# Causal attention in a two-layer block: 512-query groups per head replaced by head pairs, 256-query groups and split value and output projections

## The reference, cut to what matters

```python
qs = (x @ wq_sem).reshape(b, sl, 16, 64);  ksem = (x @ wk_sem).reshape(b, sl, 16, 64)
qg = _rope((x @ wq_geo).reshape(b, sl, 16, 64)); kg = _rope((x @ wk_geo).reshape(b, sl, 16, 64))
v = (x @ wv).reshape(b, sl, 16, 128)
g = sigmoid(gate_logit)[None, :, None, None]
scores = g * (qs . ksem) * 64**-0.5 + (1 - g) * (qg . kg) * 64**-0.5
attn = softmax(where(causal, scores, -1e9))
out = (attn @ v).reshape(b, sl, 16 * 128) @ wo
```

## Time and profile before

| | us |
|---|---|
| median of 3 runs | 1966.86 |
| profiled execution | 1968.04 |
| its span, first to last instruction | 1966.4 |
| TensorE busy | 1781.5 (91%) |
| DVE busy | 1106.4 (56%) |
| ACT busy | 972.0 (49%) |
| GpSimd busy | 802.1 (41%) |

### The profile page before, as it was taken

One profiled execution on the slowest core, in us unless ns is written; L12 is line 12 of the kernel. 1 busy time (PEld: TensorE's weight loads), 2 busy tenths in 40 slices (PEclk: granted clock), 3 DMA queues, 4 the chain that ended last, 5 costly groups with the idle time before them and its releaser, 6 DMA issues. The chain is left out here.

```text
span 1966.4 us, 33208 instructions
## 1 busy us (share of the span) xinstructions
PE 1781.5 (91%) x9018; PEld 1315.6 (67%) x9018; DVE 1106.4 (56%) x2157; ACT 972.0 (49%) x2052; POOL 802.1 (41%) x788
## 2 busy tenths in 40 slices
PE   6399988439999999999999999999999999999998
PEld 2256656427777777777777777777776677677777
DVE  4799953695546455554645454555544333334467
ACT  4599923015555555555555455555554344444322
POOL 1489931333433444343434434443432233222354
PEclk9599999559999999999999999999999999999999
DMA  4753258200000000000000000000101999999623
GB/s 138 287 183 105 98 154 261 84 3 20 9 20 16 21 8 19 16 20 7 16 21 8 19 16 21 8 19 16 39 9 31 286 313 314 308 315 321 192 87 97
DMA packets 99216, 192.94 MB, mean 98 GB/s; under 512 B 15332, under 2 KB 59620, under 8 KB 96596
## 3 DMA queue, kind: packets, MB, share of 16 engines
q1 hardware_dynamic: 57684, 108.76, 18.0%
q0 software_dynamic: 17152, 47.67, 7.5%
q10 hardware_dynamic: 24336, 35.98, 5.5%
HBM read 140.84 MB, written 51.51 MB: 98 GB/s over the span
## 5 line engine op out<-in xcount | busy, mean ns | idle before, releaser
L1175 POOL TENSOR_TENSOR sw<-sw,rope_t 64x512 f32<-64x512 f32 x128 | 164.3, 1283 | 611.9 <-ACT sw L995 611.9
L1078 DVE TENSOR_TENSOR t<-ps,rope_t 128x512 f32<-128x512 f32 x128 | 88.5, 692 | 363.5 <-ACT sw L995 363.4
L890 PE MATMUL ps<-pt,v 128*128 128x512 f32 (+3 forms) x768 | 270.1, 495 | 19.8 <-DVE xr L1095 17.8
L987 ACT ACTIVATE pb<-ps,negmax 128x128 f32<-128x128 f32 (+7 forms) x256 | 191.1, 747 | 177.1 <-DVE negmax L1063 177.0
L1063 DVE TENSOR_REDUCE negmax<-ps 128x1 f32<-128x128 f32 (+7 forms) x256 | 191.9, 750 | 78.1 <-PE ps L849 76.1
L890 PEld LDWEIGHTS ps<-pt,v 128*128 128x128 f32 x768 | 139.1, 191 | 121.4 <-issue 79.5
L541 POOL DMA_DIRECT2D w2r<-in_w x148 | 77.5, 523 | 326.1 <-PE ps L590 306.3
L1178 POOL TENSOR_TENSOR t<-t,sw 64x512 f32<-64x512 f32 x128 | 179.1, 1399 | 33.6 <-POOL sw L1175 17.9
L883 PE MATMUL ps<-ident,pb 128*128 128x128 f32 x1152 | 171.3, 276 | 23.6 <-ACT pb L987 23.4
L974 ACT COPY pt<-ps 128x512 f32<-128x512 f32 (+3 forms) x256 | 130.1, 508 | 102.0 <-PE ps L883 94.5
L883 PEld LDWEIGHTS ps<-ident,pb 128*128 128x128 f32 x1152 | 133.8, 141 | 68.1 <-ACT pb L987 45.1
(11 more groups left out here) (198 smaller groups left out, 3677.2 us busy)
## 6 DMA issues: line engine op xcount, KB each, us to landing
w13r<-in_w SPq DMA_DIRECT2D x124, 352.0 KB, 6.0
w2r<-in_w POOLq DMA_DIRECT2D x148, 176.0 KB, 6.0
result<-yy ACTq DMA_DIRECT2D x148, 128.0 KB, 5.1
crow<-c_rows SPq DMA_DIRECT2D x32, 512.0 KB, 3.6
t<-sorted SPq DMA_DIRECT2D x124, 128.0 KB, 5.5
sorted<-zeros ACTq DMA_DIRECT2D x15, 1024.0 KB, 16.9
hc<-in_w SPq DMA_DIRECT2D x24, 352.0 KB, 5.3
wraw<-in_wqkv SPq DMA_DIRECT2D x16, 384.0 KB, 3.3
```

Of the source, the lines that this page charges most:

```text
L890: last = pe.matmul(ps[:, 6, c0:512], v[:, buf, j], pt[g][:, j, c0:512], start=j == 0, stop=j == 4 * g + 3)
L987: act.activation(pb[:, qt % 2, 0:cols], ps[:, bank:bank + 2, :].rearrange("p a n -> p (a n)")[:, 0:cols], ACT.Exp, bias=negmax[:, par, qn: ...
L1175: g.tensor_tensor(sw[64:128, p % 2, :], sw[64:128, p % 2, :], rope_t[64:128, 1, (p // 2) * 512:(p // 2 + 1) * 512], ALU.mult).then_inc(s_t ...
```

## The change

- **Order.** A pair of heads is taken together: head 1 and head 2 of the first sequence, then of the second (`body(hp, c, ...)`, c = 0 to 3, hh = c % 2 is the head in the pair). There are still 32 passes of eight steps.
- **Values** are computed for a pair: four fills of bank 7, each of two token tiles by 256 columns, split, in steps 0, 1, 4 and 7 of the pair's first pass. DVE copies them out. The weights of a pair are loaded and split together.
- **Output product** for 256 queries at a time, in steps 2, 4 and 6 and in step 0 of the next pass, plain float32 as before. Its result is taken out of PSUM in two parts, `otr` by ACT and `otl` by DVE.
- **Output projection** in steps 3, 5 and 7 and in step 1 of the next pass, now split, with weights split by DVE.
- **Copies of probabilities** are all ACT's, and stand behind the next exponential instead of before it.
- **`rest`**, the low part of q and k, goes from DVE to GpSimd, interleaved with `rotate`.
- **Memory**: the ring `w2r1` shares memory with attention, so GpSimd waits for the last addition of attention before it loads there.

The core of the diff:

```diff
         def heads_loop(eng, body):
...
+            def four(hp, ends):
+                for c in range(4):
+                    body(hp, c, ends and c == 3)
...
-            def v_half(half, bank, target_b, s_fill):
-                for i in range(4):
-                    t0 = target_b * SEQ + (half * 4 + i) * P
+            def values(m, b, fill):
+
+                pe.wait_ge(s_e7, fill - 1)
+                for a in range(2):
+                    t0 = b * SEQ + (2 * m + a) * P
+                    o = ps[:, 7, a * 2 * P:(a + 1) * 2 * P]
                     for c in range(DC):
-                        last = pe.matmul(ps[:, bank, i * P:(i + 1) * P], xnT1[:, c, t0:t0 + P], wv[:, c], start=c == 0, stop=c == DC - 1)
-                last.then_inc(s_fill, 1)
+                        last = three(pe, o, xnr[:, c, t0:t0 + P], xnl[:, c, t0:t0 + P], wvr[:, c], wvl[:, c], c == 0, c == DC - 1)
+                last.then_inc(s_b7, 1)
...
+            def output(it, g, hh):
+
+                w(pe, s_e6, output_fill(it, g) - 1)
+                pe.wait_ge(s_pl, CHUNKS * it + (2, 4, 8, 12)[g])
+                hd = slice(hh * P, (hh + 1) * P)
+                for j in range(2 * g + 2):
+                    c0 = P if j == 2 * g + 1 else 0
+                    last = pe.matmul(ps[:, 6, c0:2 * P], v[:, j, hd], pt[g % 2][:, j, c0:2 * P], start=j == 0, stop=j == 2 * g + 1)
+                last.then_inc(s_b6, 1)
...
+            def project_out(it, g, slot):
+
+                pe.wait_ge(s_e6, project_fill(it, g) - 1)
                 for a in range(2):
-                    sl = slice((2 * (which % 2) + a) * P, (2 * (which % 2) + a + 1) * P)
-                    last = pe.matmul(ps[:, 6, a * D:(a + 1) * D], ot[:, sl], wo[:], start=True, stop=True)
+                    sl = slice(a * P, (a + 1) * P)
+                    last = three(pe, ps[:, 6, a * D:(a + 1) * D], otr[:, sl], otl[:, sl], wor[:, slot], wol[:, slot], True, True)
                 last.then_inc(s_b6, 1)
...
         def att_act(act):
...
                 for qt in range(8):
+                    if qt < 7 or not last:
+                        exp_tile(it, qt + 1, hh)
                     probs(it, qt)
-                    if qt < 7 or not last:
-                        exp_tile(it, qt + 1, b)
...
         def att_dve(dve):
...
-            def rest(n, p, buf):
-                dve.wait_ge(s_qr, n + 1)
-                o = (slice(None), buf, p % 2, slice((p // 2) * 512, (p // 2 + 1) * 512))
-                dve.tensor_tensor(qkl[o], t1[:, p % 2, :], qkr[o].bitcast(F32), ALU.subtract).then_inc(s_ql, 1)
...
+            def output(it, g):
+                dve.wait_ge(s_otr, 4 * it + g + 1)
+                dve.tensor_tensor(otl[:], ps[:, 6, 0:2 * P], otr[:].bitcast(F32), ALU.subtract).then_inc(s_e6, 1)
...
         def att_pool(g):
...
-            def rotate(it, p):
+            def rotate(it, p, fill):
                 n = 4 * it + p
+                w(g, s_ql, n if p == 0 else n - 1)
                 g.wait_ge(s_a7, n + 1)
...
+            def rest(it, p, buf):
+                g.wait_ge(s_rot, 4 * it + min(p + 2, 4))
+                g.wait_ge(s_qr, 4 * it + p + 1)
+                o = (slice(None), buf, p % 2, slice((p // 2) * 512, (p // 2 + 1) * 512))
+                g.tensor_tensor(qkl[o], t1[:, p % 2, :], qkr[o].bitcast(F32), ALU.subtract).then_inc(s_ql, 1)
...
                 if not last:
                     for p in range(4):
-                        rotate(it + 1, p)
+                        rotate(it + 1, p, piece_fill(2 * hp + c // 2, c % 2, p))
+                        if p:
+                            rest(it + 1, p - 1, 1 - c % 2)
+                    rest(it + 1, 3, 1 - c % 2)
...
             att_pool(g)
+            g.wait_ge(s_e6, ALL_OUTPUTS)
             experts_pool(g, R1, shared_splits(g))
```

More of the change, by code:

```diff
@@ L930, in body @@
                     if qt < 6:
-                        scores(it, qt + 2, b)
+                        scores(it, qt + 2, hh)
                     elif not last:
[L933 to L951, removed]
@@ L952, in body @@
-                    if qt == 7 and not last:
-                        pe.wait_ge(s_e6, use6(it, VHALF) - 1)
-                        v_half(1, 6, 1 - b, s_b6)
-                        pe.wait_ge(s_e7, use7(it, 4) - 1)
-                        v_half(0, 7, 1 - b, s_b7)
+                        scores(it, qt + 2, 1 - hh)
+                    if qt == 0 and not first(it):
+                        if hh == 1:
+                            pe.wait_ge(s_e7, value_fill(pair, 3))
+                        output(it - 1, 3, 1 - hh)
@@ L957, in att_pe @@
+                    if qt in PIECE and not last:
+                        p = PIECE[qt]
+                        if qt == 2 and next_b == 0:
+                            pe.wait_ge(s_ws, 2 * hp + c // 3 * 2 + (1 - hh) + 1)
+                        piece(p, next_b, 1 - hh, piece_fill(pair, hh, p))
             heads_loop(pe, body)
-            for part in range(2):
-                output1(ITS, 0, part)
-            for which, n in ((2, W2), (3, W3)):
-                project_out(which, use6(ITS, n))
+            output(ITS - 1, 3, 1)
@@ L1155, in body @@
[L1155 to L1164 removed]
+                        output(it - 1, 3)
@@ new lines, in body @@
+                    if qt == 1 and not first(it):
+                        add_out(it - 1, 3, prev_b, 1 - hh)
+                    if qt in (2, 4, 6):
+                        output(it, qt // 2 - 1)
+                    if qt in (3, 7):
+                        invert(it, qt // 7, hh)
+                    if qt in (3, 5, 7):
+                        add_out(it, qt // 2 - 1, b, hh)
+                    if qt in VALUE and hh == 0:
+                        values(VALUE[qt], value_fill(pair, VALUE[qt]))
@@ L1165, in att_dve @@
+                    if qt == 4 and c == 3 and not last_pair(hp):
+                        dve.wait_ge(s_b6, project_fill(it - 1, 3))
+                        split_wo(2 * hp + 2, 0)
+                    if qt == 4 and c == 0 and not first(it):
+                        dve.wait_ge(s_b6, project_fill(it - 1, 3))
+                        split_wo(2 * hp + 1, 1)
             heads_loop(dve, body)
-            for which, n in ((2, W2), (3, W3)):
-                add_out(which, 1, use6(ITS, n))
+            output(ITS - 1, 3)
```

349 lines of the change are left out of this document (180 added, 169 removed).

## The result

| | before | after |
|---|---|---|
| median of 4 runs, us | 1966.8 | 2187.3 |
| range, us | 1964.19 to 1968.01 | 2185.26 to 2192.23 |
| profiled execution, us (its span) | 1968.0 (1966.4) | 2192.23 (2190.6) |

The ratio is 1.1127 with a 95% interval of 1.1105 to 1.1149. The direction and the range of the prediction held; the time came out 42 us above the forecast of 2145, or 46 us with profiled executions compared (2146).

What follows compares the result with a forecast made beforehand. TensorE was taken to set the pace in attention. Terms of -0.75, -0.60, -1.3, +5.1, +2.6 and +0.65 sum to +5.7 us a pass; 31 passes make +177, the ends +1, giving a median of 2145 us, range 2060 to 2215.

Steps and rivals of the forecast that it cites:

- The wait: At step 6 the next pass's first scores wait for GpSimd's low part of piece 1: +5.1 us in 31 passes.
- X: Start of the last product of q/k piece 2 on TensorE, which was forecast to go on at X + 6.0.
- The clock: After the hole TensorE runs at half clock for 5.3 us, half of it lost: +2.6 us a pass.
- The rival in which the clock holds: Holes of 4.9 us in attention do not bring the lower clock: +3.1 us a pass, 2064 us; chance 0.14.
- The heavier rival: Each GpSimd operation in the chain is slowed, the clock spell costs 3.2: +1.95 us a pass, 2205 us; chance 0.12.
- the slow addition of the earlier trace: GpSimd addition before the change, 1.73 instead of 1.28 us, begun 0.09 us after a DVE subtraction reading SBUF.
- TensorE's savings: Split products at 0.12 us each: values -0.75 and output projection -0.60 us a pass.
- The estimate of 0.109 us: Skill's figure for a 256-column product, against 0.12 from the rows; would lower the sum by 0.5 us a pass.
- The smaller wait: At a pass's end TensorE waits 1.3 us for an exponential and ACT copies in every second pass: +0.65.
- the other idle time beside the stall: TensorE's old idle time of 1.3 us a pass, all counted as gone: -1.3.
- the splits of weights: DVE operations at step 1 before a maximum step 3 wants; one pass in four may lose 1 us; counted at nothing.
- The second expert weights: Loaded after attention instead of during it; a load takes 6.0 us to land, half counted: +3 us.

Runs made afterwards that it cites:

- Experiments 1 and 2: Changed kernel with GpSimd making piece 1's low part before starting piece 2 (1978.1 us, 1.0097), or with `rest` given back to DVE (1980.1 us, 1.0102).
- experiment 1: Changed kernel with GpSimd making the low part of piece 1 before it starts on piece 2: 1978.1 us, 1.0097 of the kernel before.
- experiment 3: Changed kernel with 18 dead products of 512 columns put on TensorE in front of the kept wait: 2127.5 us, 1.0852 of the kernel before.
- experiment 5: Changed kernel with the earlier low parts on GpSimd, and each maximum on DVE taken one step sooner: 1905.1 us, 0.9658 of the kernel before.
- pairs 9 to 12: Second expert weights loaded late (1.0015) or late in shared memory (1.0025) on the kernel before; early (0.9625) or late (0.9664) on the kernel with earlier low parts and maxima.

## Why the prediction came out as it did

**The wait** was read rightly, in place, releaser and length: X + 5.75 against X + 6.0, one hole in 31 passes of 32, released by GpSimd's subtraction. Experiments 1 and 2 show that the queue's order makes it. The subtraction took 1.28 us, the lower bound, where I took 1.35.

**The clock.** The spells were forecast at +2.6 us a pass, half of 5.3 us in each. TensorE's busy time in a pass is 34.17 us, and 31.87 in experiment 1 without a hole, so they take 2.3; experiment 3's undisturbed passes say 2.1. No pass has the 5.3 us: the spells last some 3.4 or some 6.8 us, the longer ones partly in the hole, so it is the mean that came out near. The rival in which the clock holds is out: 0.93 in the loop, and experiment 3 shows that a TensorE kept at work through the wait keeps it. The heavier rival is out too, with three GpSimd operations of 1.26 us each. GpSimd's busy time rose by 131 us, not 173: the subtractions take 162.5, and the additions fell from 179.1 to 165.0 us, in line with the slow addition of the earlier trace rows, whose neighbour on DVE is gone.

**TensorE's savings** were a little large. A value group of twelve products takes 1.52 us (1014.15 to 1015.67), not 1.44, a projection group of six 0.80, not 0.72. The timeline shows why: the first product of a group starts 0.20 us before the second, the others 0.12 (ten steps from 1014.35 to 1015.55). The estimate of 0.109 us by the Trainium skill ("TensorE: Matmul & The Clock Gate", Back-to-back issue gap), which the prediction set beside the rows, is not met here: 0.12. A pass saves 0.59 and 0.28 us where I had 0.75 and 0.60.

**The smaller wait** at the end of a pass was read rightly in place, and a little too long: 1.08 us at 1010.17, in every second pass, where no values stand between (+0.54 a pass for +0.65). In the other passes the transposes at the same place (after 1051) follow the values without a wait.

**The term that was mis-sized** is the other idle time beside the stall. I counted all of the old 1.3 us as gone, "since the stall below gives every engine time to catch up", and the splits of weights at nothing, with "one pass in four may lose 1 us" in the text and not in the sum. Measured: 1.7 us a pass beside the hole, 1.2 of it not forecast. The old waits did go; new ones came at other places. In the pass of a pair's second head TensorE waits 1.05 us at the transposes of step 5 (1071.94), for ACT's copies behind the exponential; in one pass in four 1.05 us at the transposes of step 3 (1062.89), for an exponential whose maximum stood behind the splits of weights on DVE; the rest is in waits of under 0.3 us. The stall lets the engines catch up in step 6, but these waits come of the order in DVE's and ACT's queues after it. That late maxima make most of them is shown by experiment 5, on the kernel without the hole: idle time falls from 2.4 us a pass to 0.5.

**The sum again.** A pass grew by 6.6 us, not 5.7: +0.16 and +0.32 for the savings, +1.05 for idle time, -0.25 for the hole and -0.3 for the clock, which is 6.7; the 0.1 too much is not placed. Over 31 passes that is 28 of the 46 us. The second expert weights and what follows: the experts take 337.7 us from their first product with expert weights to the end of the last, against 322.0, so +15.7 where I had +3. The wait itself is 4.4 us; the pairs 9 to 12 put the price of the late loads at 3 to 8 us. The rest is not settled: in this one trace transfers of the expert stage ran at some 300 GB/s (308 to 321 before) and their loads took 6.9 us to land, 6.0 before, but other kernels with the same placement had 324 to 334 us. The last 5 us lie in the first and last pass and outside these stretches.

## What to carry to other kernels

Before the last link of a chain is given to another engine, look at what stands in front of it in that engine's queue: an operation of 1.3 us cost 5 us a pass because it stood behind work on a piece that had not been issued, and the order alone gave it back. Count a hole in TensorE's stream with what follows it; here 4.6 us of waiting brought 2.1 to 2.3 us of lost clock, and without both the pass was 6.2 us shorter (34.3 against 40.5), as some of what was won went into other waits. And when an engine that bounds a stage shows short waits for softmax, see whether the maximum can be taken a step sooner: that one line was worth 2.7% before the change and 4.4% after it, more than the new forms of product.

## What the runs showed of the hardware

GpSimd's float32 product or subtraction takes 1.28 us for 64x512 and for 128x512 alike (L1185, L1194): twice the partitions cost nothing here.

TensorE's clock fell after single holes of 2.8 to 4.6 us, in this otherwise dense stage too, and in experiment 3 after two idle stretches, of 1.5 to 2.0 and 2.1 to 2.3 us, with some 1 us of work between. Waits of 1.05 to 1.45 us did not bring it down (clock 1.00 in experiment 1's window).

In experiment 1's row 1015.82 a DVE cast of 128x256 took 1.13 us, as did six others of the sixteen of that line; in the kernel after they have a median of 0.286. GpSimd meanwhile:

```profile
1014.19 2.62 POOL L1194 TENSOR_TENSOR qkl<-t,qkr 128x512 fp32r<-128x512 f32 x2
```

It had two of the subtractions on hand until 1016.81, and the cast ended at 1016.95. This is the reverse of the slow addition in the earlier trace rows and in line with the rule of the shared port pair in the Trainium skill ("SBUF — State Buffer", "SBUF: two separate sides"), which the prediction weighed: each of the two engines can hold up the other. No run shows what it costs the whole kernel.
